# Where the buffers of a fused attention and MLP kernel start in SBUF: small tiles grouped apart, a pad of 64 bytes, every large tile on a multiple of 512 bytes

## What is computed

```python
# layer 0, per batch (C = 128 channels, T = 512)
Mn = Wn @ inorm(x) + bn;  Mm = Wm @ inorm(ctx) + bm
A  = softmax(Mn.T @ Mm)                       # 512 x 512
x  = Wo @ (Wl @ ctx @ A.T + bl) + bo + x
# layer 1 (D = 512, 16 heads of 32, inner width 2048)
q, k, v = layer_norm(x) @ q_w + q_b, ctx @ k_w + k_b, ctx @ v_w + v_b
h   = softmax(q k.T / sqrt(32), masked) @ v @ cproj_w + cproj_b + x
out = h + gelu(layer_norm2(h) @ fc_w + fc_b) @ proj_w + proj_b
```

## The kernel before, in words

| tiles | start modulo 512, before |
|---|---|
| `ident` | 128 |
| `stage`, `rows`, `y`, `first_hi`, `first_lo`, `hid` | 160 |
| `qc_hi`, `qc_lo`, `small`, `small_t`, `small_hi`, `small_lo`, `outT_hi`, `outT_lo` | 448 |
| `v_bias`, `cproj_bias`, `at_hi`, `at_lo`, `u_hi`, `u_lo`, `x1` | 128 |
| `x_in`, `ctx_in` | 384 |
| `blocks`, `normed`, `normed_hi`, `normed_lo`, `m_hi`, `m_lo`, `ctxT_hi`, `ctxT_lo` | 32 |
| `x1b`, `x1n`, `xnT_hi`, `xnT_lo`, `k_sb`, `qT`, `kT`, `v_sb` | 256 |
| `rest_hi`, `rest_lo`, `proj_bias`, `yT`, `yT_hi`, `yT_lo`, `gl`, `hT_hi`, `hT_lo` | 448 |

## Time and profile before

### The profile page before, as it was taken

One profiled execution on the slowest core, in us unless ns is written; L12 is line 12 of the kernel. 1 busy time (PEld: TensorE's weight loads), 2 busy tenths in 40 slices (PEclk: granted clock), 3 DMA queues, 4 the chain that ended last, 5 costly groups with the idle time before them and its releaser, 6 DMA issues. The chain is left out here.

```text
span 3179.3 us, 56992 instructions
## 1 busy us (share of the span) xinstructions
PE 3101.0 (98%) x18551; PEld 2564.7 (81%) x18551; DVE 1957.9 (62%) x3965; ACT 1354.1 (43%) x3954; POOL 815.5 (26%) x738
## 2 busy tenths in 40 slices
PE   4999999999999999999998899999999999999999
PEld 3788888888888888888887688888888888888887
DVE  4888888888888888888885533333333333333332
ACT  2566666666666666666666311111111111111111
POOL 2444444444444444444442200000000000000000
PEclk8999999999999999999999999999999999999999
DMA  3111111111121111111112211111111111111110
GB/s 100 44 51 50 50 50 50 50 50 50 53 56 53 50 50 50 50 50 50 50 44 63 99 40 40 40 40 40 28 25 40 35 31 40 40 40 40 40 27 14
DMA packets 342418, 147.59 MB, mean 46 GB/s; under 512 B 286177, under 2 KB 286689, under 8 KB 342369
## 3 DMA queue, kind: packets, MB, share of 16 engines
q1 hardware_dynamic: 342368, 146.96, 17.4%
HBM read 97.57 MB, written 33.55 MB: 41 GB/s over the span
## 5 line engine op out<-in xcount | busy, mean ns | idle before, releaser
L1155 ACT ACTIVATE gl<-pre,fc_bias 128x512 f32<-128x512 f32 x256 | 176.6, 690 | 1128.0 <-PE pre L1240 1128.0
L1194 DVE CAST hT_hi<-gl 128x512 fp32r<-128x512 f32 x256 | 109.0, 426 | 847.5 <-ACT gl L1155 847.5
L605 ACT ACTIVATE rows<-bank,negmax 128x128 f32<-128x128 f32 x1024 | 362.9, 404 | 88.3 <-DVE negmax L791 88.3
L1239 PE MATMUL pre<-yT_hi,rest_lo 128*128 128x512 f32 x768 | 299.2, 390 | 0.0
L1238 PE MATMUL pre<-yT_lo,rest_hi 128*128 128x512 f32 x768 | 299.0, 389 | 0.0
L1240 PE MATMUL acc<-rest_hi,hT_hi 128*128 128x512 f32 x768 | 298.9, 389 | 0.0
L1240 PE MATMUL pre<-yT_hi,rest_hi 128*128 128x512 f32 x768 | 298.8, 389 | 0.0
L1238 PE MATMUL acc<-rest_lo,hT_hi 128*128 128x512 f32 x768 | 298.8, 389 | 0.0
L1239 PE MATMUL acc<-rest_hi,hT_lo 128*128 128x512 f32 x768 | 298.8, 389 | 0.0
L506 POOL TENSOR_TENSOR rows<-rows,rsum 128x512 f32<-128x512 f32 x256 | 258.7, 1042 | 18.8 <-DVE rsum L688 18.8
L856 PEld LDWEIGHTS bank<-ident,rows 128*128 128x128 f32 x2048 | 235.9, 143 | 22.6 <-ACT rows L605 3.7
(11 more groups left out here) (159 smaller groups left out, 7380.9 us busy)
## 6 DMA issues: line engine op xcount, KB each, us to landing
x_in<-in_x SPq DMA_DIRECT2D x64, 256.0 KB, 2.6
ctx_in<-in_ctx SPq DMA_DIRECT2D x64, 256.0 KB, 2.9
blocks<-in_ctx SPq DMA_DIRECT2D x1024, 16.0 KB, 2.0
small<-in_x SPq DMA_DIRECT2D x64, 256.0 KB, 3.3
hidden<-hid SPq DMA_DIRECT2D x64, 256.0 KB, 2.0
rows<-hidden SPq DMA_DIRECT2D x16, 1024.0 KB, 5.6
out<-rows SPq DMA_DIRECT2D x64, 256.0 KB, 2.1
stage<-y SPq DMA_DIRECT2D x240, 64.0 KB, 2.3
```

What stands on the lines that cost most here:

```text
L605: act.activation(probs[:, r, c, :], by_chunk(S1_BANK[r])[:, c, :], ACT.Exp, bias=negmax1[:, r, c:c + 1], accum_out=sum1[:, r, c:c + 1]).th ...
L1155: act.activation(gl[:, i % 2, :], pre[i % 2][:], ACT.Gelu_apprx_tanh, bias=mlp.fc_bias[:, i:i + 1]).then_inc(gelu_done, 1)
L1239: pe.matmul(out, a_lo, b_hi, start=False, stop=False)
```

## The change

Only the order of the allocations changes, and one unused tile of 64 bytes is added. In `Handover` the small tiles come first, then the pad, then `ident` and the large tiles. In `attention_pass` the small tiles go behind all the large ones; `outT_hi` and `outT_lo` go ahead of them. No instruction, wait, DMA or loop is added, removed or moved.

```diff
+PAD = 16
...
-        self.ident = sb("ident", [P, P])
         self.neghalf = sb("neghalf", [P, TILES])
-        self.stage = sb("stage", [P, 2, STAGE, 512])
...
         self.ln_vecs = sb("ln_vecs", [P, 2, 4])
         self.fc_bias = sb("fc_bias", [P, 16])
         self.stats = sb("stats", [P, TILES, 6])
         self.mv = sb("mv", [P, TILES, 2])
         self.ve = sb("ve", [P, TILES])
         self.rstd = sb("rstd", [P, TILES])
+        sb("pad", [P, PAD])
+        self.ident = sb("ident", [P, P])
+        self.stage = sb("stage", [P, 2, STAGE, 512])
+        self.rows = sb("rows", [P, 2, TILES, 512])
+        self.y = sb("y", [P, TILES, 512])
+        self.first_hi = sb("first_hi", [P, 2, STAGE, 512], F32R)
+        self.first_lo = sb("first_lo", [P, 2, STAGE, 512], F32R)
+        self.hid = sb("hid", [P, 2, 512])
...
-        vecs = sb("vecs", [P, 4, DC])
-        q_scale = sb("q_scale", [P, DC])
...
         v_sb = sb("v_sb", [P, 2, D])
+        outT_hi = sb("outT_hi", [P, DC, P], F32R)
+        outT_lo = sb("outT_lo", [P, DC, P], F32R)
+        vecs = sb("vecs", [P, 4, DC])
+        q_scale = sb("q_scale", [P, DC])
...
```

More of the change, by code:

```diff
@@ L99, in __init__ @@
         self.rstd = sb("rstd", [P, TILES])
+        sb("pad", [P, PAD])
[6 more added lines that the diff above has]
+        self.hid = sb("hid", [P, 2, 512])
+        self.y_chunks = self.y[:].rearrange("p c (t b) -> p c t b", b=P)
         self.hid_stored = [sem(f"hid_stored{i}") for i in range(2)]
@@ L193, in attention_pass @@
         small_lo = sb("small_lo", [P, 3, P], F32R)
-        vecs = sb("vecs", [P, 4, DC])
-        q_scale = sb("q_scale", [P, DC])
-        bias0 = sb("bias0", [P, 4])
-        out0_bias = sb("out0_bias", [P, 1])
-        q_bias = sb("q_bias", [P, DC])
         v_bias = sb("v_bias", [P, D])
         cproj_bias = sb("cproj_bias", [P, D])
-        masked_bf = sb("masked_bf", [P, P], BF16)
         x_in = sb("x_in", [P, 2, T])
         ctx_in = sb("ctx_in", [P, 2, T])
[L206 to L209, removed]
         x_res = small[:].rearrange("p a b -> p (a b)")
@@ L219, in attention_pass @@
         ctxT_lo = sb("ctxT_lo", [P, DC, P], F32R)
-        negmax0 = sb("negmax0", [P, DC])
-        sum0 = sb("sum0", [P, DC])
-        rsum0 = sb("rsum0", [P, DC])
         at_hi = sb("at_hi", [P, DC, T], F32R)
@@ L227, in attention_pass @@
         x1 = sb("x1", [P, D])
[L229 to L232, removed]
         x1b = sb("x1b", [P, 2, D])
@@ L241, in attention_pass @@
         v_sb = sb("v_sb", [P, 2, D])
+        outT_hi = sb("outT_hi", [P, DC, P], F32R)
+        outT_lo = sb("outT_lo", [P, DC, P], F32R)
+        vecs = sb("vecs", [P, 4, DC])
+        q_scale = sb("q_scale", [P, DC])
+        bias0 = sb("bias0", [P, 4])
+        out0_bias = sb("out0_bias", [P, 1])
+        q_bias = sb("q_bias", [P, DC])
+        masked_bf = sb("masked_bf", [P, P], BF16)
+        in_stats = sb("in_stats", [P, 2, 6])
+        in_mv = sb("in_mv", [P, 2, 2])
+        in_ve = sb("in_ve", [P, 2])
+        in_rstd = sb("in_rstd", [P, 2])
+        negmax0 = sb("negmax0", [P, DC])
+        sum0 = sb("sum0", [P, DC])
+        rsum0 = sb("rsum0", [P, DC])
+        x1_stats = sb("x1_stats", [P, 6])
+        x1_mv = sb("x1_mv", [P, 2])
+        x1_ve = sb("x1_ve", [P, 1])
+        x1_rstd = sb("x1_rstd", [P, 1])
         mask_u8 = sb("mask_u8", [P, 2, P], U8)
@@ L246, in attention_pass @@
         rsum1 = sb("rsum1", [P, 4, 4])
-        outT_hi = sb("outT_hi", [P, DC, P], F32R)
-        outT_lo = sb("outT_lo", [P, DC, P], F32R)
         sp_steps = sem("sp_steps")
```

## The result

The changed kernel takes 3154.93 us (median of 4 runs, 3153.84 to 3155.92) against 3180.36 for the kernel before: a ratio of 0.9921, with a 95% interval of 0.9904 to 0.9938. That is 25.4 us less, where 32.5 were forecast; the sign, the cause and the range (3138 to 3163) held. The profiled execution took 3153.84 with a span of 3152.1, so the two spans are 27.2 us apart.

The account below looks back on a forecast made before the run. TensorE's instruction stream was taken as the bound; 11.5 us from the second pass plus 21.8 from the first gave 33.3, taken as 32.5, so 3181.1 - 32.5 - 0.9 = 3148 us, range 3138 to 3163.

Parts of the forecast that it names:

- The second pass: Matmuls touching `first` (unequal remainders, 396 to 398 ns) come down to `rest`'s 389 or 390: 11.5 us gained.
- The first pass: Large matmuls with unequal remainders drop to the equal-pair level: 341 ns in each of 64 batches, 21.8 us.
- U: First pass, `at` with `ctxT`: 12 matmuls per batch go from 397 to 389 ns, saving 96 ns.
- Q: First pass, `qc` with `xnT`: 12 matmuls per batch go from 394 to 389 ns, saving 60 ns.
- M: First pass, `normed` with `small`: 6 matmuls per batch go from 397 to 389 ns, saving 48 ns.
- K and V: First pass, `first` with `ctxT`: 8 triples per batch fall from 1207 to 1191 ns, saving 128 ns.
- C and S0: First pass, `qc` with `outT` and `m` with `m`: remainders already equal, so a gain of 0.
- Transposes: 44 a batch, 2816 in all, streaming `ident`: no change expected, bounded at 8.4 us less or more.
- The slot's turn: First pass: `hid` and `m_lo` end 0.37 and 0.43 us early; about 0.3 us should remain, leaving TensorE the bound.
- the rival by which another engine would become the bound: First pass keeps 26.00 us a slot, for instance because ACT holds it back; only the second gains: 3169; 7 in 100.
- the traffic of a group's turn: Second pass: DMA traffic, not layout, slows matmuls with `first`, so the change does nothing: 3180; 8 in 100.
- Slower transposes: `ident` starting at the same remainder as its partners makes reads collide; at 20 ns each, 3204 us; 3 in 100.

Follow-up runs that it names:

- e1: Changed kernel without its 64-byte pad, so all large tiles start at 448 modulo 512 with distances still 0: 3154.36 us, ratio 0.9915.
- e2: Changed kernel with a pad of 96 bytes instead of 64, so all large tiles start at 32 modulo 512: 3155.51 us, ratio 0.9921.
- e3: Kernel before plus one 224-byte pad putting the second pass's tiles at 160 like `first`, first pass untouched: 3169.99 us, ratio 0.9965.
- e4: Changed kernel with `yT` (and `gl`) moved to 32 and `hT` to 64 modulo 512, second-pass weights at 0: 3192.0 us, one execution.
- e5: Changed kernel with `yT` (and `gl`) moved to 256 and `hT` to 128 modulo 512, second-pass weights at 0: 3181.99 us, one execution.

## Why the prediction was right, and where it was off

**The bound and the cause: right.** TensorE's stream sets the time, and it got shorter without any instruction being removed. That the difference of the starts counts and not the remainder is shown by e1, e2 and e3, and by e4 and e5 from the other side. That the starts are compared modulo 512 was more than the rows could say: at 256 e5 shows the step of an equal pair.

**The second pass: right.** 11.5 us were forecast; e3 measured 11.5. The traces, from the first `pre` to the last `acc`, give 11.0: 1409.96 us before, 1398.94 after. So near a hit is in part luck, for two small errors cancel. The means of `pre` with `first` in the earlier trace rows hold the matmuls at a low clock at the head of the pass; by steps a matmul with `first` gained 6.7 ns and not 7.5, 10.2 us in all. And `rest` behind each run with `first`, put at nothing, gave the other 0.8.

**The first pass: the term that was mis-sized.** 341 ns a slot were forecast, and 245 came (mean slots of 26.007 and 25.762 us). By form, with the means of all three passes before and after: U gained 92 where 96 were forecast, Q 64 where 60, M 46 of 48, out0 6 of 9. K and V gained 8 x (1207 - 1198) = 72 where 128 were forecast. C and S0, for which I had written 0, lost 4 x 6 = 24 and 4 x 4 = 16. The sum is 240. The failing step is the one by which I took `qc` with `outT` of the kernel before (1191 a triple) as what any equal pair behind a transpose costs. It was a favourable case: that pair settled after two long steps there, and settles after nine now. Nor do all triples with `first` follow transposes: half of them follow the scores. (341 - 240) x 64 is 6.5 us, most of the 7.1 by which 32.5 was too much.

**Transposes: right at 0.** 272 ns in all kernels, at distances of 0, 32, 128 and 256 between `ident` and `rows`. What I left out is that they cost something through the matmuls behind them.

**The slot's turn: right.** The timeline after, in the form of the earlier trace rows:

```profile
1013.74 0.69 DVE L694 TENSOR_TENSOR hid<-bank,x1b 128x512 f32<-128x512 f32 x1 [0.50 <-PE bank L826]
...
1014.76 1.91 PE L855 MATMUL bank<-ident,rows 128*128 128x128 f32 x16
1015.04 1.41 DVE L700 SCALAR_TENSOR_TENSOR m_lo<-bank,bias,m_hi 128x512 fp32r<-128x512 f32 x2 [0.40 <-ACT m_hi L562]
...
1016.86 0.48 PE L824 MATMUL bank<-m_lo,m_hi 128*128 128x512 f32 x1
```

`hid` ends 0.33 us before the transposes that wait for it (0.37 before), and `m_lo` 0.41 before S0 (0.43 before). The slack stayed, so the rival by which another engine would become the bound did not come.

**The other rivals.** That the traffic of a group's turn slows the matmuls is refuted by the window with 0.32 of DMA share at 226.7 ns a step. Slower transposes did not come either.

**The page.** The Trainium skill, "SBUF — State Buffer", section "Who interferes with whom", gives TensorE two independent read ports, one for the moving operand and one for weight loads, and says that it never waits on anyone. As a rule for the time of this kernel it does not hold: e4 differs from the changed kernel by two pads of 32 bytes and takes 37 us longer. Where in the SBUF the two reads meet, no run here shows.

## What to carry to other kernels

Where a stream of float32 matmuls with a new weight load each sets the time, look at where the moving tile and the next weights start modulo 256 bytes (a common remainder modulo 512 gives that too). If two forms of one shape differ by some ns in the profile, sort them by that difference; giving all large tiles one remainder, which one did not matter among 0, 32 and 448, cost here no instruction and gave 0.8%. Before you call the mean of a form a price, look at its steps in order: in e5 means up to 5 ns too long came from the neighbours of a group, and not from its own placement. When you take a baseline for such a sum from the trace, do not take it from a form that stands behind another kind of work unless the change leaves that work's neighbours alone: how long the stream takes to settle is not a property of the form.

## What the runs showed of the hardware that was not expected

The step between two float32 matmuls of 512 columns with a new weight load each is 226.7 ns when the moving tile and the next weights start at the same remainder, and 5 to 8 ns more on average at distances of 32, 64, 96, 128, 192 and 288 bytes (288 is `first` with `yT`, before). 256 bytes cost nothing once the steps have settled: 227 ns in e5.

Equal starts do not give the short step at once. After a run of transposes or of an unequal pair the steps pass through one fixed series (235, 233, 236, 224, 231, 236, 228, 232, 231, 227 ns), entered at different points, and then stay at 227. In the second pass this made even `rest` a little slow before, for the first five matmuls behind each run with `first`. Why the series is what it is, and what sets the entry, stays open.
